# Last stage without GpSimd: VectorE subtracts the low parts of every unit's activations

## The reference, cut to what matters

```python
xf = x.reshape(T, D)                                  # T=4096 tokens here, D=128
shared = jax.nn.silu(xf @ Ws_up) @ Ws_down            # F=64
aff = xf @ centroids.T                                # E=64 experts
...                                                   # top 8, sigmoid, normalised: cw[T, E]
h = jax.nn.silu(jnp.einsum('td,edf->etf', xf, W_up))  # W_up [64, 128, 64]
y = jnp.einsum('etf,efd->etd', h, W_down)             # W_down [64, 64, 128]
routed = jnp.einsum('etd,te->td', y, cw)
return (shared + routed).reshape(B, S, D)
```

## Time and profile before

| what | value |
|---|---|
| median of 3 runs (lowest, highest) | 1243.56 us (1239.83, 1243.59) |
| the profiled execution: its own time | 1238.93 us |
| the profiled execution: span in the trace | 1237.2 us |
| mean granted TensorE clock, as a share of full speed | 0.922 |
| busy over the span: PE, PEld, DVE, ACT, POOL | 82%, 65%, 70%, 57%, 37% |
| POOL's low parts (L650), 128 of them | 167.5 us busy, 1309 ns mean |
| DVE's low parts (L1473), 136 of them | 94.4 us busy, 694 ns mean |
| DVE's products (L1466), 256 of them | 174.0 us busy, 680 ns mean |

### The profile page before, as it was taken

One profiled execution on the slowest core, in us unless ns is written; L12 is line 12 of the kernel. 1 busy time (PEld: TensorE's weight loads), 2 busy tenths in 40 slices (PEclk: granted clock), 3 DMA queues, 4 the chain that ended last, 5 costly groups with the idle time before them and its releaser, 6 DMA issues.

```text
span 1237.2 us, 20735 instructions
## 1 busy us (share of the span) xinstructions
PE 1012.8 (82%) x6214; PEld 801.6 (65%) x6260; DVE 863.4 (70%) x1963; ACT 701.0 (57%) x1313; POOL 458.9 (37%) x500
## 2 busy tenths in 40 slices
PE   2573099999148899899898846999999999999998
PEld 1353099999126666666666635777777777767676
DVE  2888367777447778778776536868686878786765
ACT  2443055555226667666666434767676676676765
POOL 0177700000675454554543232333333333333333
PEclk9765599999569999999999977999999999999999
DMA  8011112222201001001000000000000000000000
GB/s 229 11 43 41 67 55 65 61 65 59 62 11 30 21 22 31 19 24 29 18 27 10 1 1 1 1 6 4 10 1 9 1 10 0 9 0 9 1 10 9
DMA packets 56571, 33.51 MB, mean 27 GB/s; under 512 B 16128, under 2 KB 54432, under 8 KB 56480
## 3 DMA queue, kind: packets, MB, share of 16 engines
q1 hardware_dynamic: 52384, 23.96, 7.0%
q0 software_dynamic: 4096, 8.40, 2.2%
HBM read 20.73 MB, written 11.60 MB: 26 GB/s over the span
## 4 chain that ended last, share of the span: by engine, by line
PE 62%; DVE 10%; ACT 9%; POOL 5%; issue 5%; DMA 0%; POOLq 0%; DVEq 0%; ACTq 0%; SPq 0%
PE ps L1862 5%; PE ps L1841 5%; PE ps L1864 5%; PE ps L1863 5%; PE ps L1842 5%; PE ps L1843 4%; PE ps L1850 4%; ACT pt L767 3%; DVE nm L1288 3%; POOL xs L520 3%; PE ps L1626 3%; PE ps L1592 2%; PE ps L1593 2%; PE ps L1685 2%; PE ps L1573 2%
## 5 line engine op out<-in xcount | busy, mean ns | idle before, releaser
L650 POOL TENSOR_TENSOR hl<-h,hh 128x512 fp32r<-128x512 f32 x128 | 167.5, 1309 | 318.3 <-ACT hh L889 318.3
L1466 DVE TENSOR_TENSOR h<-sg,ps 128x512 f32<-128x512 f32 x256 | 174.0, 680 | 110.1 <-ACT sg L877 108.7
L877 ACT ACTIVATE sg<-ps 128x512 f32<-128x512 f32 x256 | 153.3, 599 | 100.5 <-PE ps L1843 99.6
L889 ACT ACTIVATE hh<-h 128x512 fp32r<-128x512 f32 (+1 forms) x264 | 165.2, 626 | 13.7 <-DVE h L1466 13.3
L1288 DVE TENSOR_REDUCE nm<-ps 128x4 f32<-128x512 f32 (+1 forms) x128 | 116.6, 953 | 36.8 <-PE ps L1667 36.3
L1850 PE MATMUL ps<-cwT,selr 128*128 128x512 f32 x256 | 103.5, 404 | 16.7 <-DVE h L1466 16.5
L1862 PE MATMUL ps<-hh,wh 128*128 128x512 f32 x256 | 102.6, 401 | 2.5 <-POOL hl L650 1.0
L1841 PE MATMUL ps<-xh,wh 128*128 128x512 f32 x256 | 103.7, 405 | 0.0
L1473 DVE TENSOR_TENSOR hl<-h,hh 128x512 fp32r<-128x512 f32 (+1 forms) x136 | 94.4, 694 | 12.0 <-ACT hh L889 12.0
L1842 PE MATMUL ps<-xl,wh 128*128 128x512 f32 x256 | 101.8, 398 | 0.0
L767 ACT ACTIVATE pt<-ps 128x1536 f32<-128x1536 f32 x64 | 92.4, 1444 | 15.7 <-PE ps L1647 15.7
(11 more groups left out here) (300 smaller groups left out, 2695.3 us busy)
## 6 DMA issues: line engine op xcount, KB each, us to landing
xb<-xs SPq DMA_DIRECT2D x72, 64.0 KB, 1.8
ys<-yb SPq DMA_DIRECT2D x72, 64.0 KB, 1.6
x_res<-in_L_attn_x_dram SPq DMA_DIRECT2D x4, 512.0 KB, 6.0
wst<-in_L_ffn_W_up_dram SPq DMA_DIRECT2D x32, 64.0 KB, 2.2
wst<-in_L_ffn_W_down_dram SPq DMA_DIRECT2D x32, 64.0 KB, 1.9
out_dram<-y SPq DMA_DIRECT2D x8, 256.0 KB, 2.3
stg<-in_L_ffn_Wg_dram SPq DMA_DIRECT2D x1, 1584.0 KB, 12.2
stu<-in_L_ffn_Wu_dram SPq DMA_DIRECT2D x1, 1584.0 KB, 16.2
```

Source lines behind the costliest of these rows:

```text
L650: pool.tensor_tensor(hl4[:, u % 3, :], h4[:, u % 3, :], hh4[:, u % 3, :].bitcast(F32), op=ALU.subtract).then_inc(u_hlp, 1)
L877: act.activation(sg4[r, u % 3, :], bank[u % 3][r, :], ACT.Silu).then_inc(u_sg, 1)
L889: act.activation(hh4[r, u % 3, :], h4[r, u % 3, :], ACT.Copy).then_inc(u_hh, 1)
L1466: dve.tensor_tensor(h4[:, u % 3, :], sg4[:, u % 3, :], bank[3 + u % 2][:, :], op=ALU.mult).then_inc(u_h, 1)
```

## The change

The code of POOL for the last stage is taken out, and its semaphore `u_hlp` with it. `e_lo` on DVE no longer returns early for odd units, so that it makes the low part of each of the 33 units of a tile. `is_split` now waits for one counter, `u_hl`, in steps of one per unit.

```diff
-        u_hlp = sem("e_hl_pool")
...
             if u < 0:
                 t, u = t - 1, NU + u
-            if u % 2:
-                eng.wait_ge(u_hlp, t * (NU // 2) + u // 2 + 1)
-            else:
-                eng.wait_ge(u_hl, t * (NU - NU // 2) + u // 2 + 1)
+            eng.wait_ge(u_hl, t * NU + u + 1)
...
-            def pool_tile(t, p, before, N, S):
-                for u in range(1, NU, 2):
-                    pool.wait_ge(u_hh, t * NU + u + 1)
-                    apart(pool, pool_passed)
-                    pool.tensor_tensor(hl4[:, u % 3, :], h4[:, u % 3, :], hh4[:, u % 3, :].bitcast(F32),
-                                       op=ALU.subtract).then_inc(u_hlp, 1)
-
-            tiles_of(pool, pool_tile)
...
             def e_lo(t, u):
-                if u % 2:
-                    return
                 r = slice(0, F2 if u == 0 else P)
                 dve.wait_ge(u_hh, t * NU + u + 1)
                 dve.tensor_tensor(hl4[r, u % 3, :], h4[r, u % 3, :], hh4[r, u % 3, :].bitcast(F32),
```

## The result

The changed kernel takes 1245.83 us in the median of 11 runs (1244.14 to 1249.72), the kernel before, on the same chip and in the same rounds, 1243.23 us (1239.20 to 1243.82). The ratio is 1.0036, 95% interval [1.0022, 1.0051]: slower by 4.5 us, between 2.7 and 6.3. That goes with the means, 1246.6 and 1242.1; the medians are only 2.6 us apart. The profiled execution took 1245.12 us with a span of 1243.4, 6.2 us more than before.

The account below looks back on a forecast made before the run. PE was taken as the bound, with DVE next. Terms 7.1 - 0.65 + 0.5 = +7.0 us on the profiled 1238.93 gave 1245.9, or 1250.5 with the median's 4.6 added; range 1243 to 1256.

Parts of the forecast that it names:

- What bounds, and where to look: Last stage: PE bounds, DVE has some 13 us to spare a tile; look at DVE's backlog in units 17 to 22.
- Relief of DVE's steps: Routing steps L1448, L1437 and L1426 on DVE shorten with POOL silent, by 1.11, 0.88 and 0.56 us a tile.
- the 0.56 us of L1426: Routing step on DVE ahead of unit 22's product: shorter by 0.56 us a tile; without it the sum is 3.9 us higher.
- Units 17 to 22, +1.02 a tile: Added low parts delay unit 22's product and unit 21's down matmul: +1.0 us in seven tiles, +7.1 us in all.
- it does not move: Unit 17's product starts at 968.91, when silu comes from ACT, and was claimed to stay there after the change.
- The tail, -0.65: End of the last tile: DVE makes unit 31's low part sooner than POOL, -0.65 us, bounds -1.0 to 0.
- The jump, +0.5: Loop's jump back: DVE's last instruction ends 0.6 us later, PE stops once, +0.5 us, bounds 0 and 0.6.
- Other places at nothing: Low parts elsewhere, such as units 1 to 16, end before PE wants them: cost nothing, covered by DVE's idle time.
- The level of 1250.5: Forecast median: 1245.9 us plus the 4.6 by which the old kernel's median exceeded its profiled execution.
- the absorbed case: Rival: low parts of units 17, 19 and 21 fit DVE's slack, only the tail counts: 1242.9 us, chance 0.23.
- DVE as the bound over all steps of units 17 to 28: Rival: six odd low parts, 3.6 us a tile, all land on PE, +25 us: 1268.8, chance 0.07.
- Faster: Rival: low parts ready earlier on DVE (0.68 against 1.29 us) remove PE's stops, -8.4 us: 1235.2, chance 0.05.

Follow-up runs that it names:

- experiment 1: Changed kernel, but POOL keeps the low parts of units 17, 19 and 21: ratio 0.9998 [0.9983, 1.0013] to the kernel before.
- experiment 2: Kernel before, but DVE takes over the low parts of units 17, 19 and 21 alone: ratio 1.0059 [1.0036, 1.0082].
- experiment 6: Changed kernel, but POOL keeps unit 31's low part of every tile: one profiled execution, last stage 487.85 us, jump tile 60.86 us.
- experiment 7: Changed kernel with routing steps of units 17 to 19 in unit 16 and ACT's weights copy moved from unit 28 to 30: 1235.18 us, ratio 0.9865.
- experiment 5: Changed kernel plus an unused POOL subtraction of the same size after each odd unit's high part: ratio 1.0233 [1.0154, 1.0312], last stage 511.64 us.
- experiments 1 to 4: POOL keeping low parts 17, 19, 21; only those moved to DVE; routing steps early in changed kernel; same in kernel before: ratios 0.9998, 1.0059, 0.9973, 0.9992.
- experiments 5 to 10: POOL reading beside DVE; POOL keeping unit 31; ACT's weights copy later in four versions, three with early routing steps: ratios 1.0233, none, 0.9865, 0.9893, 0.9876, 0.9896.

## Why the prediction was right, and where its size was off

The forecast was slower with 0.67; measured was slower by 0.36%. It gave +7.0 us; the last stage got 5.56 us longer and the ratio says 4.5 [2.7, 6.3]. The place and the mechanism were right; the sum was 1.4 us too high, 0.9 of it in the tiles. The 5.56 us are made up so: seven tiles +6.20, the jump +0.34, behind the last product -0.83, ahead of the first logits -0.15.

- **What bounds, and where to look**: held. PE stayed the bound, and experiments 1 and 2 show the loss to lie in three low parts of sixteen. The other thirteen were costed at nothing, and cost nothing in the units where they stand (unit 31's costs at the jump, which has its own term).
- **Relief of DVE's steps**: held, 1531 to 419 ns and two more. The sum took the 0.56 us of L1426, and the product of unit 22 came at the hundredth forecast with it.
- **Units 17 to 22, +1.02 a tile**: the mechanism held, and the size nearly did in the tiles outside the loop: 60.85 - 59.90 = 0.95, 60.85 - 59.86 = 0.99, and +0.93 from the logits of tile 6 to the last product (1140.27 to 1228.37 before, 1146.37 to 1235.40 after). This is the mis-sized term: in the four tiles of the loop it was 0.82 to 0.84. The step that failed is "it does not move", of the product of unit 17. The kernel before had a delay there that the changed one has not: in the loop, silu ended at 968.80 and the product began at 968.91; in the changed kernel silu ended at 972.06 and the product began at 972.09. The same again at the product released by silu of unit 29: 990.91 to 991.03 before, 995.09 to 995.12 after. In all four loop tiles it is 0.11 to 0.13 us at these two places before and 0.03 or 0.04 after, and in the tiles outside the loop it is 0.03 or 0.04 in both kernels. The other products of the loop that DVE stood waiting for silu with show the same, but it is these two that PE waits for. Two times 0.08 us make up the 0.15 by which the kernel before's tiles are longer in its loop (60.01 against 59.86) and the changed kernel's are not (60.85 in both). The backlog was worked out from a loop tile, where this hides. What causes the delay stays open. The silu of unit 17, the kernel before in a loop tile, then the changed one:

```profile
968.20 0.60 ACT L877 ACTIVATE sg<-ps 128x512 f32<-128x512 f32 x1
```

```profile
971.46 0.60 ACT L863 ACTIVATE sg<-ps 128x512 f32<-128x512 f32 x1
```

- **The tail, -0.65**: measured -0.64 at the down matmul of unit 31. The prediction had the low part of unit 32 done in time, and it wasn't quite: the weight load behind waited 0.26 us for it, and 0.54 us of the gain was left when ACT copied the result out. At the end of the span it was -0.83, though: behind the issue of the last output the kernels in which DVE makes unit 31's low part need 2.70 to 2.80 us to the end of the span, those in which POOL makes it 3.00 to 3.08. The cause was not looked for.
- **The jump, +0.5**: measured +0.34 over the neighbours, and shown to be unit 31's in experiment 6 (it is 0.66 in experiment 1 and 0.57 in experiment 7).
- **Other places at nothing**: held. The 0.15 us ahead of the first logits (25.09 to 24.94 us from the stage's first matmul) is within what kernels with the same instructions up to there show, 24.61 to 25.09.
- The level of 1250.5 is 4.7 us above the measured median, more than the difference's error of 1.4 to 2.5. The prediction added the 4.6 us by which the kernel before's median lay above its profiled execution, and the changed kernel's median lay only 0.7 above its own (1245.83 and 1245.12): the kernel before's runs lie near 1239.5 and near 1243.5, its median on the upper ones, while the profiled runs of both kernels lie low in their own sets.
- **Rivals**: the absorbed case fell with experiment 2, DVE as the bound over all steps of units 17 to 28 with experiment 1, where the low parts of units 23, 25 and 27 are on DVE and the tiles stay at 59.8 to 60.0 us. "Faster", for which the rule of the Trainium skill ("GPSIMD Engine Reference", section "4.1 Engine selection") spoke, elementwise work on VectorE, came true only at the tail: a single low part is there sooner, but not one that stands behind a backlog. The Trainium skill's rule on the port ("SBUF — State Buffer", section "Who interferes with whom"), that a VectorE instruction with two SBUF inputs and a GpSimd instruction that reads SBUF exclude each other, was borne out by experiment 5 with 1.59 against 0.68 us.

## What to carry to other kernels

An engine with 13 us to spare in 60 can still lose when work is moved onto it: what counts is the stretch in which it runs without a gap, found by following its queue from the last wait to the next instruction that somebody waits for. Before moving work between engines, look for what is queued behind somebody else's wait: taking three routing steps into DVE's idle time and one copy two units later took 15.6 us off the stage with POOL kept and 15.7 with all low parts on DVE, so that their place was then worth nothing. And a helper engine's work must be priced with what it costs its neighbour: the relief, 0.56 us, was half as much as the 1.20 us put in at the place that decided.

## What was not expected of the hardware

When POOL ran beside low parts on DVE, no routing step of the tile was slowed: the low parts bore it, 987 ns in the mean against 684, and up to 1.71 us. It is no particular instruction that loses, but one that stands in line when POOL starts.

In tiles of the loop the product began 0.11 us after silu in the kernel before and 0.03 us after the changed one's. The kernels in which POOL makes three or more of the low parts have longer tiles in the loop than outside, by 0.06 to 0.18 us, and there the delay of 0.11 to 0.13 us where a product was waiting for silu; those with all low parts on DVE or with unit 31's alone on POOL have neither (experiment 5's longer tiles in the loop come without the delay: 0.03 us). The cause was not looked for.

The time ahead of the last stage, with code that the change does not touch, differs between executions and chips: the stage began at 755.0 to 759.3 us in the traces of both kernels and of experiments 1 to 4, and at 764.5 to 775.0 in those of experiments 5 to 10, on two other chips.
